# A gated MoE attention kernel on one core: the first gates spread ahead of the weights' scales, and the first pass reordered around them

## What is computed

```
x = x + tanh(g_xattn) * softmax(LN(x) Wq (ctx Wk)^T / sqrt(128)) (ctx Wv)     # 77 context tokens, per sequence
x = x + tanh(g_ffn)   * ffn(LN(x))
ffn(h): logits = normalised(h) @ normalised(sim) - sigmoid(gates)             # 16 experts
        w      = softmax over the experts with logits > 0 (the two best, if none is)
        q, k, v = sum_e w[:, e] * (h @ proj_e)      # for each of q_proj, k_proj, v_proj
        o      = softmax(q k^T / sqrt(128)) v       # within each sequence's 128 tokens
        out    = sum_e w[:, e] * (o @ o_proj_e)
```

## Time and profile before

| what | value |
|---|---|
| median of 3 runs | 800.32 us (799.54 to 801.37) |
| profiled execution | 799.99 us |
| its span | 798.1 us |
| mean granted TensorE clock | 0.987 of full speed |
| PE / DVE / POOL / ACT busy | 97% / 76% / 61% / 54% |

### The profile page before, as it was taken

One profiled execution on the slowest core, in us unless ns is written; L12 is line 12 of the kernel. 1 busy time (PEld: TensorE's weight loads), 2 busy tenths in 40 slices (PEclk: granted clock), 3 DMA queues, 4 the chain that ended last, 5 costly groups with the idle time before them and its releaser, 6 DMA issues.

```text
span 798.1 us, 13995 instructions
## 1 busy us (share of the span) xinstructions
PE 776.1 (97%) x3999; PEld 418.1 (52%) x3999; DVE 607.2 (76%) x2037; ACT 433.8 (54%) x1129; POOL 483.0 (61%) x703
## 2 busy tenths in 40 slices
PE   7489999999999999999999999999999999999998
PEld 6445545555455555545555554555555455544444
DVE  2977787878787787778777787877878786775648
ACT  5554645556555655655565565456556555544445
POOL 3276657674746757474675747567574755765534
PEclk9789999999999999999999999999999999999999
DMA  6564476563655636365563636546364654543100
GB/s 192 136 216 159 162 219 174 169 209 94 209 161 164 189 106 204 97 210 167 151 191 106 202 109 209 166 150 186 101 207 116 208 160 139 163 135 116 53 14 28
DMA packets 97476, 122.57 MB, mean 154 GB/s; under 512 B 14611, under 2 KB 69111, under 8 KB 97399
## 3 DMA queue, kind: packets, MB, share of 16 engines
q1 hardware_dynamic: 96679, 121.59, 49.6%
q10 hardware_dynamic: 720, 0.08, 0.1%
HBM read 97.32 MB, written 24.31 MB: 152 GB/s over the span
## 4 chain that ended last, share of the span: by engine, by line
PE 88%; DVE 5%; DMA 2%; POOL 1%; ACT 1%; issue 1%; SPq 0%; DVEq 0%; ACTq 0%; POOLq 0%
PE acc_q L1380 20%; PE acc_k L1380 20%; PE acc_v L1380 20%; PE y L1409 9%; PE oT_p L1409 9%; PE m L1489 2%; PE m L1553 2%; DVE x_all L1175 1%; PE oT_p L1641 1%; PE m L1480 1%; PE m L1539 1%; DMA stage<-in_L_ffn_q_proj_dram 1%; PE m L1469 1%; POOL zq L658 1%; PE m L1529 1%
## 5 line engine op out<-in xcount | busy, mean ns | idle before, releaser
L658 POOL TENSOR_TENSOR zq<-zq_full,zq 128x512 f16<-128x512 f32 x256 | 297.8, 1170 | 222.4 <-ACT zq L743 222.2
L743 ACT ACTIVATE zq<-zq_full 128x512 f16<-128x512 f32 x256 | 160.1, 636 | 224.1 <-DVE zq_full L1145 224.0
L1175 DVE SCALAR_TENSOR_TENSOR x_all<-y,w_out,x_all 128x128 f32<-128x128 f32 x356 | 122.2, 343 | 96.1 <-issue 69.5
L1380 PE MATMUL acc_q<-zq,w_hi 128*128 128x512 f16 x510 | 193.3, 379 | 1.0 <-POOL zq L658 1.0
L1380 PE MATMUL acc_k<-zq,w_hi 128*128 128x512 f16 x510 | 193.2, 379 | 0.0
L1380 PE MATMUL acc_v<-zq,w_hi 128*128 128x512 f16 x510 | 193.2, 379 | 0.0
L1145 DVE TENSOR_TENSOR zq_full<-wq_bc,x2T_p 128x512 f32<-128x512 f32 x256 | 167.8, 668 | 2.5 <-DMA wq_bc<-w_rows 1.7
L1175 DVE SCALAR_TENSOR_TENSOR x_all<-oT_p,w_out,x_all 128x128 f32<-128x128 f32 x356 | 121.5, 341 | 0.0
L673 POOL TENSOR_TENSOR x_all<-stage,x_all 128x128 f32<-128x128 f32 x240 | 100.4, 456 | 19.8 <-DVE x_all L1175 13.3
L1380 PE MATMUL acc_q<-zq,w_lo 128*128 128x512 f16 x255 | 96.6, 379 | 0.0
L1380 PE MATMUL acc_v<-zq,w_lo 128*128 128x512 f16 x255 | 96.6, 379 | 0.0
(11 more groups left out here) (253 smaller groups left out, 1091.4 us busy)
## 6 DMA issues: line engine op xcount, KB each, us to landing
wq_bc<-w_rows SPq DMA_DIRECT2D x128, 512.0 KB, 4.5
blk_rows<-stage SPq DMA_DIRECT2D x26, 256.0 KB, 2.7
stage<-blk_rows SPq DMA_DIRECT2D x104, 64.0 KB, 2.0
blk_rows<-v_blk SPq DMA_DIRECT2D x15, 256.0 KB, 2.0
v_mix<-blk_rows SPq DMA_DIRECT2D x60, 64.0 KB, 2.9
blk_rows<-pc_blk SPq DMA_DIRECT2D x15, 256.0 KB, 4.1
pcT<-blk_rows SPq DMA_DIRECT2D x60, 64.0 KB, 2.0
out_dram<-x_all SPq DMA_DIRECT2D x15, 256.0 KB, 6.7
```

The source lines that it names most:

```text
L658: nc.gpsimd.tensor_tensor(zq[:, 1, e % Z_SLOTS, :], zq_full[:, e % F_SLOTS, :], zq[:, 0, e % Z_SLOTS, :], ALU.subtract).then_inc(zq_lo_poo ...
L743: nc.scalar.activation(zq[:, 0, e % Z_SLOTS, :], zq_full[:, e % F_SLOTS, :], ACT.Copy).then_inc(zq_hi_done, 1)
L1175: nc.vector.scalar_tensor_tensor(out=rows(x_all, g, b0 + b), in0=bank[:, tok(j)], scalar=w_out[:, g % 2, e, b0 + b:b0 + b + 1], in1=rows(x ...
L1380: last = nc.tensor.matmul(acc[m][:], w[:, m, s, :], zq[:, half, s % Z_SLOTS, :], start=(s == 0 and n == 0), stop=(s == E - 1 and n == 2))
```

## The change

- q_proj is loaded first, then the three extra contexts, K, x(1), V, O, x(2).
- The gates of group 0 are computed ahead of V's maximum and of the scales. Of their spreading, the first pair goes as two transfers, one for each expert (`wq_first_in` for expert 0).
- The high and low parts of Q, K and V are made in three parts of 4, 6 and 6 experts (`PARTS`); PE waits for a part at its first expert. Parts 0 and 1 are in the head but for `weight_low(V, 1)`, which stands in step 0, and parts 2 stand in steps 1 to 3 (ACT) and 3 to 5 (DVE).
- The first attention of group 0 goes ahead of the extra contexts on PE and ACT; `att_product(1)` goes from the head to behind expert 0, `x1_add(1)` and `second_stats(1)` to DVE's step 0, `first_stats(2)` to its step 2.
- POOL: `second_rstd(1)` goes to step 2, `second_norm(1)` and `first_rstd(2)` to step 3. ACT: `x2_norm(1)` goes to step 3, `x_norm(2)` to step 4. `late(0)` goes from 1 to 3, so x2's transpose is after step 5 and the logits in step 7; `xn_transpose(2)` stays after step 6.
- O's maximum goes from step 2 to 10, its gather from 4 to 11, its spread from 7 to 12, its high part from 9 to 14 and its low part from step 11 to pass 1, step 3.
- `oT_high(0)` is taken ahead of `zq_high` in its step. xnT of group 0, 1, 2 uses banks m0, acc_q, m1. `keep_busy` is called in more places, 20 matmuls in all behind the first one's 8 instead of 8.

```diff
-        MAX_AT, SHARE_AT = (0, 2), ((0, 4), (0, 7))
-        HIGH_AT = (0, 9)
-        LOW_AT = (0, 11)
+        MAX_AT, SHARE_AT = (0, 10), ((0, 11), (0, 12))
+        HIGH_AT = (0, 14)
+        LOW_AT = (1, 3)
...
 SP head
+                load_weights(Q, q_proj)
                 sp.dma_start(zq_full[0:S, 0:PRE]..., c_v[:, G:G * (PRE + 1), :]).then_inc(ctx_pre_in, 16)
-                load_weights(Q, q_proj)
                 load_weights(K, k_proj)
+                load_x(1)
                 load_weights(V, v_proj)
-                load_x(1)
...
+                for e, done in enumerate((wq_first_in, wq_in[0])):
+                    src = w_rows[0:1, G * e:G * (e + 1), :].rearrange("a r n -> (a r n)")
+                    sp.dma_start(wq_bc[:, 0, e], src.partition_broadcast(P)).then_inc(done, 16)
-                for j in range(W_SLOTS):
+                for j in range(1, W_SLOTS):
...
 POOL: head, then body
-                for e in range(LEAD - 1):
+                for e in range(LEAD):
                     zq_low(0, e)
-                second_rstd(1)
-                zq_low(0, LEAD - 1)
-                first_rstd(2)
+                    if i == 0 and s == 2:
+                        second_rstd(1)
                     for g, e in zq_at(i, s):
                         zq_low(g, e)
-                    if s == 1 and i < 2:
+                    if s == (3 if i == 0 else 1) and i < 2:
                         second_norm(g2)
+                    if i == 0 and s == 3:
+                        first_rstd(2)
...
 ACT head, its end
+                x_exps(1)
+                weight_high(Q)
                 weight_high(K)
-                x_exps(1)
+                weight_high(V)
+                zq_high(0, 0)
                 pxT_out(1)
-                weight_high(V)
-                for e in range(LEAD):
-                    zq_high(0, e)
+                zq_high(0, 1)
+                weight_high(Q, 1)
+                weight_high(K, 1)
+                zq_high(0, 2)
+                weight_high(V, 1)
+                zq_high(0, 3)
 ACT body
+                    if i == 0 and s == 3:
+                        x2_norm(1)
                     for g, e in zq_at(i, s):
                         zq_high(g, e)
-                    if s == (3 if i == 0 else 0) and has(g1):
+                    if s == (4 if i == 0 else 0) and has(g1):
                         x_norm(g1)
...
 DVE head, from weight_max(K)
+                first_stats(1)
                 setup_gate()
-                weight_max(V)
-                share_largest(0)
-                first_stats(1)
-                weight_scales(0)
                 x2_norm_inverse(0)
                 gate_logits(0)
                 gate_mask(0)
                 gate_softmax(0)
+                weight_max(V)
+                x_max(1)
+                share_largest(0)
+                weight_scales(0)
                 weight_low(Q)
-                x_max(1)
                 weight_low(K)
                 x_sum(1)
                 zq_scale(0, 0)
+                weight_low(V)
                 zq_scale(0, 1)
-                weight_low(V)
                 zq_scale(0, 2)
-                x1_add(1)
-                second_stats(1)
                 zq_scale(0, 3)
-                first_stats(2)
+                weight_low(Q, 1)
+                weight_low(K, 1)
 DVE body, behind zq_scale
+                    if i == 0 and s == 0:
+                        x1_add(1)
+                        second_stats(1)
+                        weight_low(V, 1)
+                    if i == 0 and s == 2:
+                        first_stats(2)
+                    if i == 0 and s in (3, 4, 5):
+                        weight_low((Q, K, V)[s - 3], 2)
...
 PE head, its end
                 for b in range(G):
                     small_product(-1, 9 - sooner(-1), b)
+                keep_busy(3)
+                gather_max(0, acc[V])
+                pe.wait_ge(vx_sb, PRE + 1)
+                spread_max(0, acc[K])
+                keep_busy(2)
                 px_transpose(1)
-                att_product(1)
+                keep_busy(6)
```

More of the change, by code:

```diff
@@ L40 @@
 PRE = 3
+PARTS = ((0, 4), (4, 10), (10, 16))
+GATES_LATE = 3
 GATE_STEPS = 12
@@ L411, in vx_bank, with split_part @@
             return (acc[V], oT_p, acc[K])[g - 1] if 1 <= g <= PRE else m0
+        def split_part(t, m, part):
+            experts = slice(*PARTS[part]) if m < O else slice(0, E)
+            return t[:, m, experts].rearrange("p e h -> p (e h)")
         def ctx_slot(g):
@@ L733, in values_weight, with weight_high @@
                 nc.scalar.activation(exp_0[:], tanh_f[:], ACT.Exp)
-            def weight_high(m):
+            def weight_high(m, part=0):
                 act.wait_ge(scales_done, 1 if m < O else 2)
-                nc.scalar.activation(w_hi[:, m], stage[:, m], ACT.Copy,
+                nc.scalar.activation(split_part(w_hi, m, part), split_part(stage, m, part), ACT.Copy,
                                      scale=w_up[:, m:m + 1]).then_inc(hi_done[m], 1)
@@ L811, in xnT_out @@
                     wait(act, xnT_ps, g + 1)
-                    nc.scalar.activation(xnT[:], (acc[Q] if g == 1 else m0)[:], ACT.Copy).then_inc(xnT_sb, 1)
+                    nc.scalar.activation(xnT[:], (m0, acc[Q], m1)[g][:], ACT.Copy).then_inc(xnT_sb, 1)
                 else:
@@ L877, in pxT_out, with oT_high @@
                                          px_mix[:].rearrange("p i b n -> p b i n"), ACT.Copy).then_inc(pxT_sb, 1)
+            def oT_high(g):
+                wait(act, oT_ps, g + 1)
+                wait(act, y_ps, PAIRS_Y * (g - 1))
+                nc.scalar.activation(oT[:, g % 2, 0, :], oT_p[:], ACT.Copy).then_inc(oT_hi_done, 1)
             def head():
@@ L889, in head @@
                 vx_out(0)
-                ctxT_out(1)
                 pxT_out(0)
[L892 to L896, removed]
+                for g in range(1, PRE + 1):
+                    ctxT_out(g)
+                for g in range(1, PRE):
                     kxT_out(g)
@@ L928, in body @@
                         y_scale(gd, 7, banks=(1,))
+                    if i == 1 and s == Y_FIRST:
+                        oT_high(0)
+                    if i == 0 and s == 3:
+                        x2_norm(1)
                     for g, e in zq_at(i, s):
@@ L971, in body @@
                         kxT_out(g1)
-                    if s == Y_FIRST and has(gc):
-                        wait(act, oT_ps, gc + 1)
-                        wait(act, y_ps, PAIRS_Y * (gc - 1))
-                        nc.scalar.activation(oT[:, gc % 2, 0, :], oT_p[:], ACT.Copy).then_inc(oT_hi_done, 1)
+                    if s == Y_FIRST and i > 1 and has(gc):
+                        oT_high(gc)
                     if s == 10 - sooner(i) and has(g1):
@@ L1376, in experts @@
                 for m in (Q, K, V):
+                    for part, (first, _) in enumerate(PARTS):
+                        if (i, s) == (0, first):
+                            pe.wait_ge(hi_done[m], part + 1)
+                            pe.wait_ge(lo_done[m], part + 1)
                     if s == 0:
@@ L1506, in xn_transpose @@
                     wait(pe, kxT_sb, 2)
-                wait(pe, logit_read, cap(g))
+                if g == 2:
+                    wait(pe, x1_done, 2)
                 for b in range(G):
-                    last = nc.tensor.transpose((acc[Q] if g == 1 else m0)[:, tok(b)], xn[:, b, :], ident[:])
+                    last = nc.tensor.transpose((m0, acc[Q], m1)[g][:, tok(b)], xn[:, b, :], ident[:])
                 last.then_inc(xnT_ps, 1)
@@ L1574, in head @@
                 vx_product(0)
+                px_transpose(0)
+                att_product(0)
                 for g in range(1, PRE + 1):
                     ctx_transpose(g)
-                px_transpose(0)
-                kx_product(1)
-                att_product(0)
-                vx_product(1)
-                for g in range(2, PRE + 1):
+                for g in range(1, PRE + 1):
                     kx_product(g)
@@ L1618, in body @@
                         scores(gc, i)
+                    if i == 0 and s == 0:
+                        att_product(1)
                     if s == 2 + late(i) and g2 < X2_HEAD:
```

38 lines of the change are left out of this document (23 added, 15 removed).

## The result

The changed kernel takes **808.88 us** (median of 4 runs, 808.06 to 810.58), the kernel before 800.83 us (799.54 to 801.37) beside it: a ratio of 1.0106, 95% interval 1.0083 to 1.0128. It is slower by 8.0 us, where 3.7 us were forecast, and the time lies above the range (797.6 to 806.6). The profiled execution took 809.48 us, 9.5 us more than that of before.

A forecast was written before the change was run, and what follows sets the result against it. PE, busy 97% of the span, bounds the kernel; only what lies ahead of about 105 us counts. Terms -4.8 + 2.7 + 0.9 + 1.9 + 1.4 + 1.0 + 0.6 = +3.7 on 799.99 give 803.7 us, range 797.6 to 806.6.

The forecast's parts named there:

- (1)-(3): Head: Q first and gates early bring the first product to 37.15 us from 41.36; 4.8 us gained at expert 1.
- (4): Experts 1 to 6: POOL's chain delays group 2's norm; PE stands 4.5 us, its transpose only 2.1 us early.
- (5): Behind group 2's transpose: group 1's logits, gather_max(1) and a wait give PE 0.9 us more.
- (6): Behind expert 11: PE waits 1.2 to 2.7 us at gather_max(1) for O's maximum; 1.9 us lost.
- (7): Behind expert 12: spread_max(1) waits for share_largest(1) on DVE, 0.6 to 2.1 us; 1.4 us lost.
- (8): Pass 1, step 3: weight_low(O) on DVE makes oT_low later; 1.0 us lost, between 0 and 2.3.
- (9): Behind the 4.5 us stop for group 2's norm: PE's clock may halve; 0.6 us lost, bounds 0 and 1.3.
- rival A: Whole kernel: stalls as worked out from the queues' order; 803.7 us, range 801.5 to 806.5; chance 0.50.
- Rival B: Head's gain survives if POOL has first_rstd(2) by expert 6's end; 796.0 us, 794.5 to 798.4; chance 0.20.
- Rival D: POOL's subtractions are stretched beside DVE's w_lo parts, +2.4 us or more; 806 to 809 us; chance 0.07.
- C: Norm's stall stands, but O's maximum and its spread are met; 800.4 us, 798.4 to 801.7; chance 0.18.
- E: Head: two half spreads take as long as the pair, first gates slip 1 to 3 us; 801 to 806; chance 0.05.

The follow-up runs named there:

- e2: Changed kernel with O's maximum, share, high and low parts back at the steps of the kernel before: 805.1 us, ratio 1.0064.
- e11: Changed kernel with POOL's roots early (as e1) and the head's gaps filled (as e7): 801.24 us, ratio 1.0012.
- e8: Changed kernel with the edits of e7, e1 and e2 together: 796.59 us, ratio 0.9952.
- e7: Changed kernel with 26 more small matmuls in PE's short idle times between 9 and 17 us: 808.47 us, ratio 1.0094.
- e3: Changed kernel with the three w_lo parts for experts 10 to 15 all in DVE's step 6: 808.55 us, ratio 1.0099.
- e1: Changed kernel with POOL's second_rstd(1) ahead of expert 5's subtraction and first_rstd(2) ahead of expert 7's and second_norm(1): 804.68 us, ratio 1.0049.
- e9: e7 with keep_busy(18) added ahead of xn_transpose(2), in PE's stop: 806.24 us, ratio 1.0076.
- b1: Kernel before, with small matmuls filling PE's gaps in the head: 800.29 us against 800.34, ratio 1.0.
- e10: e8 with the first pair of gate rows in one transfer, as in the kernel before: 796.17 us, ratio 0.9954.
- e6: Changed kernel with the edits of e1 and e2, without the filled head: 798.78 us, ratio 0.9986.
- c0: The changed kernel run again with nothing edited: 810.92 us, ratio 1.0119.
- e4: Changed kernel with 28 calls (56 instructions) of small identity matmuls ahead of xn_transpose(2): 810.67 us, ratio 1.0123.

## Why the prediction was right or wrong

By the profiled executions (forecast, then measured, us on the time):

```
(1)-(3) head to expert 1            -4.8    -4.0
(4)     to xn_transpose(2)          +2.7    +6.0
(5)     more work behind it         +0.9    +1.0
(6)     O's maximum                 +1.9    +2.1
(7)     its spread                  +1.4    +1.3
(8)     pass 1                      +1.0    +0.9
(9)     clock behind the stop       +0.6    +2.3
sum                                 +3.7    +9.6
```

The measured sum is against 9.5 us; 0.1 is rounding. (4) is 5.95 of the result's section; (5) is what is left of the 6.6 us behind the transpose; (9) is the 4.37 us from 63.90 to 68.27 that expert 7 takes with its logits, less the 2.55 it would take at 0.216 a matmul, and 0.5 more for the transposes (0.91 us to the next matmul against 0.44).

Right: the side, and the mechanism of rival A. Each wait stands at the operation where the prediction put it, the norm, O's maximum and the spread, some 4 to 7 us later in time, and within 0.2 us in size for (6) and (7). e2 (3.8 us) bears out (6) to (8) together, priced at 4.3. That the step from e11 to e8 is 4.65 us is in part luck: the stop for O's maximum is 3.5 us in e11 and not 1.9, and its clock costs more behind it. The loss of (8) shows as a wait of 1.7 us for `xnT` at L1521 of pass 1, gone in e2, while the 1.0 us for `oT` shrinks to 0.2; 0.9 us are what the end sees.

**The step that failed is (4).** It had the right chain and summed it too short, +2.7 against +6.0 us. `x_norm(2)` ended at 62.94 and not at 58.85, 4.1 us later, and the transpose with it; 0.8 of this had been lost by expert 1 and stands in the line of (1) to (3), the other 3.3 are the miss of (4). The bill, piece by piece: 1.4 us come from the first product, at 38.54 and not 37.15, with the clock at 0.50 from 10 to 15 us and 0.84 from 15 to 20 (e7, with 1.00 in both, has it at 37.01). About 1.0 come from DVE's parts and the copy and subtraction behind them: the two low parts of 768 columns took 2.12 us, 1.06 each, where the prediction had 0.85 for one, so `x1_add(1)` was at 44.62 and not 42.6, and the next part took 1.19. The root that was priced at 1.9 us took 2.9, `second_norm(1)` 2.2 and not 1.6, both beside DVE's low parts: 1.0 and 0.6. PE also stood 2.26 us for the x2 transpose of group 1, one expert ahead, which the step had not charged, since it let PE go through experts 1 to 6 unhindered. This wait does not move the end, as POOL's chain sets the later transpose (in e3 it is 1.0 us shorter and the stop 1.0 us longer). e1 and e11 show that the cause is the order on POOL: with the roots moved up, both waits are gone or 0.8 us, and the time falls by 6.6 to 7.2 us with the same filled head.

**The second is (9)**, where only the size was off: 0.6 was taken between 0 and 1.3. The profile after shows 2.3 us, and e9 gives 1.4 to 2.6 back. The bound was drawn from six matmuls at double 0.216 us, and the engine stayed at half clock for a whole expert, its logits and the transposes ahead.

The range had no room for these two. That of rival A was drawn from the bounds of (6) to (9) alone (taken all together they give 800.6 to 807.2, of which it took the inner part), and (4), the longest chain of the sum, had one value and no bounds. Two slips in the sums, 30.65 for 30.58 in (2) and 10.1 for 10.2 in (6), change nothing.

**An assumption that no step named** is a head at full clock. In the first gates' new place DVE waits for PE's logits, so the clock in the head now reaches the first product; before, it did not (b1). No step charged a second price for the stop at O's maximum either. The changed kernel's profiled execution does not pay it, e11's does.

Rival B's mechanism was right as a condition: with POOL's root in time and O's maximum early it forecast 796.0 us, and e8 takes 796.59. It was not the case of this kernel. The nearness is partly luck, as the 796.0 still hold the 1.0 us of (8), which e8 also takes back, and no filled head. Rival D is a part of the answer: 1.6 us of stretching on POOL's chain, seen in e3 and not removed by moving the parts once. Its range, 806 to 809, holds the measured 808.88, but by its own term it can have given no more than these 1.6 of the 5.2 us above the forecast; how much of it reaches the end is not shown. Rivals C and E are out: C by the waits of 2.1 and 1.3 us at O's maximum and its spread, which it took to be met, E by e10.

What stays open: e7 gains only 0.4 to 2.4 us on the changed kernel by two sets of its runs, 2.2 between e6 and e8 and 3.4 between e1 and e11; of the executions without a profile only the mean clock is on record, so the shares of the head's clock and of the clock behind the stops can't be split in a median.

## What to carry to other kernels

When work is made earlier, redo the queues that it now passes: here 4 us won at the head met a POOL order in which the change itself had put both roots behind more subtractions, and the waits that this order held took more than the gain, part of it through the clock. Put the short operations on which a critical transpose depends ahead of the long ones that only fill a buffer: moving one group of four operations up by a step, and another to the front of its step, gave about 7 us. Charge a stop of several us on PE with what comes behind it at half clock as well as its length, and hold the head's clock fixed with a few small matmuls before comparing effects of 1 or 2 us; a stop further on can still make single runs differ, as in e11.

## What the runs showed of the hardware

- The clock granted in the first 25 us differs between executions of one program: 0.84 and 1.00 in one, 0.63 and 0.69 in another, with the logits 2.05 us apart. 13 more calls of small matmuls made it 1.00 from 5 to 25 us in five profiles, with the logits at most 0.7 us apart.
- The column of the clock can miss a fall: in e3 it is 1.00 from 10 to 15 us, yet the eight matmuls of the cross scores took 1.99 us, as at 0.50 in the kernel after; in e7, at 1.00, they took 1.12.
- After a stop of 5.0 us PE was at 0.50 from 62 to 66 us, and at 0.55 from 66 to 68; from 68.06 on a matmul took 0.38 us, as at full clock, with expert 7 run in between. After shorter stops it fell in some executions and not in others: after 2.3 us to 0.50 in c0 and not in the kernel after; after 3.5 us in e1 and e11, after 2.4 in e9, after 2.1 in e4, and not after 2.1 in the kernel after. With small matmuls of the identity in the stop it stayed at 1.00 (e4, e9), even though 1.0 us of idling remained in e9.
- The small matmuls took 0.114 us each one behind another (6.41 us for 56), and each call made two.
- A POOL operation on 4 columns takes 0.23 or 1.04 us by itself and 0.82 or 1.60 beside DVE's two-input low parts; one on 512 columns 1.16 and 1.57.
